# 24 short steps of spare transpositions among the last two backs, with another table of step orders, in a four-pair transformer kernel on one core

## The reference

```
x += L0_xattn(context)       one head
x += L0_ffn                  8 attention heads; their value and output products are
                             mixed from 8 experts a head, 2 of them with a gate above 0
x += L1_xattn(context)       16 heads of 8 columns, causal and length masks
x += L1_ffn                  ternary weights, gelu, layer norm inside
x += L2_xattn(context)       2 heads of 64, per-head norms, mask
x += L2_ffn                  8 experts of 256, best 2 by a softmax gate
x += L3_xattn(context)       16 heads of 64, with a bias
x += L3_ffn                  8 small experts, best 2 by group, and a shared branch
```

## Time and profile before

| | |
|---|---|
| median of 3 runs | 689.33 us (687.62 to 689.4) |
| the profiled execution's own time | 687.04 us |
| its span, first to last instruction | 685.7 us |
| mean granted TensorE clock | 0.979 of full |
| PE busy | 647.0 us (94%) |
| DVE busy | 521.0 us (76%) |
| ACT busy | 371.8 us (54%) |
| POOL busy | 201.1 us (29%) |
| DMA | 113.86 MB, mean 166 GB/s |

### The profile page before, as it was taken

The page is one execution under the profiler, slowest core; times in us unless marked ns, Lnnn a source line. Parts: engine busy times, 40 slices in busy tenths (PEclk is TensorE's granted clock), DMA queues, the critical chain, the costliest instruction groups (busy, mean ns, idle before and its releaser), DMA issues.

```text
span 685.7 us, 14701 instructions
## 1 busy us (share of the span) xinstructions
PE 647.0 (94%) x5494; PEld 582.2 (85%) x5494; DVE 521.0 (76%) x1433; ACT 371.8 (54%) x1261; POOL 201.1 (29%) x244
## 2 busy tenths in 40 slices
PE   6789999899999999999999999999999998788987
PEld 5669999798999999898799999878899987567866
DVE  1887678886888878987788898985688776556856
ACT  2252321355665846154665586386648452865693
POOL 0000012542251222513514242144336332432040
PEclk9799999999999999999999999999999999799989
DMA  8969969896324616895334126380565400000000
GB/s 317 393 233 302 391 237 322 282 363 208 136 93 139 205 47 212 262 325 195 129 124 161 65 65 246 127 275 14 179 232 178 150 9 5 1 1 1 1 1 13
DMA packets 37656, 113.86 MB, mean 166 GB/s; under 512 B 9041, under 2 KB 11729, under 8 KB 37201
## 3 DMA queue, kind: packets, MB, share of 16 engines
q1 hardware_dynamic: 37584, 112.92, 47.0%
HBM read 111.86 MB, written 1.05 MB: 165 GB/s over the span
## 4 chain that ended last, share of the span: by engine, by line
PE 80%; DVE 10%; ACT 4%; POOL 2%; DMA 2%; issue 1%; DVEq 0%
PE bank L461 34%; PE e_bank L461 33%; PE p_bank L461 5%; PE bank L706 4%; ACT wide_b L1129 1%; DVE gated L1435 1%; DMA gated<-gates_of 1%; PE bank L695 1%; DVE x L1438 1%; DVE wide_b L1438 1%; POOL wide_b L1339 1%; DVE f_route L1435 1%; ACT f_b L1038 1%; PE p_bank L561 1%; DVE max_neg L1721 1%
## 5 line engine op out<-in xcount | busy, mean ns | idle before, releaser
L461 PE MATMUL e_bank<-weights,gated 128*128 128x128 f32 x2048 | 245.2, 276 | 0.9 <-ACT f_a L988 0.7
L461 PEld LDWEIGHTS e_bank<-weights,gated 128*128 128x128 f32 x2048 | 236.2, 192 | 7.7 <-issue 3.0
L1129 ACT ACTIVATE wide_b<-wide_b,max_neg 128x120 f32<-128x120 f32 x272 | 103.5, 386 | 21.8 <-DVE max_neg L1721 15.2
L1339 POOL TENSOR_TENSOR wide_b<-wide_b,row_inv 128x480 f32<-128x480 f32 x64 | 75.2, 1180 | 135.1 <-DVE row_inv L1726 135.0
L1435 DVE TENSOR_TENSOR gated<-gated,f_v 128x1024 f32<-128x1024 f32 x64 | 80.0, 1272 | 10.8 <-ACT f_v L988 6.2
L1435 DVE TENSOR_TENSOR gated<-gated,f_xnT 128x1024 f32<-128x1024 f32 x64 | 80.9, 1286 | 5.4 <-DMA gated<-gates_of 4.8
L988 ACT ACTIVATE wide_a<-bank 120x512 f32<-120x512 f32 (+4 forms) x110 | 58.5, 542 | 41.4 <-PE bank L706 20.6
L1331 POOL TENSOR_TENSOR rstd<-var_eps,w_const 128x1 f32<-128x1 f32 (+1 forms) x48 | 32.0, 667 | 159.6 <-DVE var_eps L1431 159.6
L1129 ACT ACTIVATION_READ_ACCUMULATOR wide_b<-wide_b,max_neg 128x1 f32 x272 | 52.1, 192 | 0.0
L706 PE MATMUL bank<-w_const,wide_b 128*120 128x128 f32 x256 | 42.4, 297 | 5.9 <-POOL wide_b L1339 5.8
L1721 DVE TENSOR_REDUCE max_neg<-wide_b 128x4 f32<-128x480 f32 x64 | 41.8, 653 | 2.2
(11 more groups left out here) (263 smaller groups left out, 1208.5 us busy)
## 6 DMA issues: line engine op xcount, KB each, us to landing
gated<-gates_of SPq DMA_DIRECT2D x128, 512.0 KB, 6.0
weights<-in_experts SPq DMA_DIRECT2D x64, 512.0 KB, 6.5
w_L2f<-in_L2f SPq DMA_DIRECT2D x1, 2124.0 KB, 14.6
w_L3x<-in_L3x SPq DMA_DIRECT2D x1, 2108.0 KB, 18.5
wide_b<-in_raw0f SPq DMA_DIRECT2D x1, 1024.0 KB, 8.1
w_L3f<-in_L3f SPq DMA_DIRECT2D x1, 1000.0 KB, 20.8
w_L1f<-in_L1f SPq DMA_DIRECT2D x1, 516.0 KB, 10.6
x_next<-in_x SPq DMA_DIRECT2D x4, 128.0 KB, 4.0
```

Of the source, the lines that this page charges most:

```text
L461: return nc.tensor.matmul(o, lhsT, rhs, start=first, stop=last)
L1129: last = nc.scalar.activation(p, p, ACT.Exp, bias=max_neg[lane][:, h:h + 1], accum_out=row_sum[lane][:, h:h + 1])
L1339: nc.gpsimd.tensor_tensor(p3, p3, row_inv[lane][:, 4 * i:4 * i + 4].unsqueeze(2).broadcast_to([128, 4, K]), ALU.mult).then_inc(probs_norme ...
```

## The change

The TensorE front stream gets 25 further steps behind pair 3's front: one that waits for `e_x_ready` of pair 3, and 24 that each issue three transpositions of the identity into `e_bank`. Nothing reads them. The order table is replaced on all five engines.

```diff
+SPARE = 24
@@ TensorE, front_steps
                     for pair in range(PAIRS):
                         yield from front_pair(pair)
+                    pe.wait_ge(e_x_ready.sem, e_x_ready.upto(L0F, 1, PAIRS - 1))
+                    yield
+                    for _ in range(SPARE):
+                        for c in range(3):
+                            nc.tensor.transpose(e_bank[:, 128 * c:128 * c + 128], ident, ident)
+                        yield
@@ ORDER["PE"], from the last front product on
-1001010101110111011011001010101101101100100110001011100101100000000010101010010101110000101001011101101001110011
+1f0f1001001110ff1f1f11011011001010101101101f1fff001001010ff0f0f1f111001f01101000000000101010010101101f00f0100101f0f101101f1f110011f00ff11
@@ ORDER["SP"]
-"ppfffpffffffffffpfffffffffffffffffffffppfffffpffffffffffffffffffffffffpfffffffpfff0fffffpfffffffff1f"
-"ffffffff0fffffffpf1ff0ffffffffffff11f0ffpfff0fffffffffffffffff1ff0011f"
+"ppffpffffffffpffffffffffffffffffpffffpfffffffffffffpffffffffffffff0f1ffpffpfffffffffffffffffffpfff"
+"ffffffff10ffffff1fpffff0ffffpfffffffffffff0ffff1f1fffff0fffffff0011fff"
...
```

More of the change, by code:

```diff
@@ L43 @@
 ORDER = {
[L44 to L67, removed]
+    "PE": "pppp0pp00pp0pppp0pp00pp0pppp0pffpffpfpfffpfffpf0pffffpfpfpfpfpffffpfffffpffffpfffpp0p101p0pfffpf1f0f"
+          "f0fp10f0f0fp000p0f0f0fff01f00f0p10f0pfp0f0p0101f10p001010010110001pf0110p10f1010f10ff1p1f10ff100p1f1"
+          "101110101f01p10010111fp1ff1pfp001p110p101f0f1f01f1f0ff1f0pf11fff1p01ff1ff10pf1f0f1f01pf0f10010p1001p"
+          "11p01f10110f0011p11f1p10f0f11p100p0f1f01f001p001001000101010100f1p10f1f1011f01pf00f010p0100110101pf1"
+          "0fp01101f0f1010f1f1f01f10p10f00f0000f0f11f00f1001100f01f011001f10f11f0110010010101f00f110f010f0001f1"
+          "1f111101f11f101f111f0010f0101f0f10101101f111f0110ff1f0f1001001110ff1f1f11011011001010101101101f1fff0"
+          "01001010ff0f0f1f111001f01101000000000101010010101101f00f0100101f0f101101f1f110011f00ff11",
@@ new lines @@
+    "Activation": "ppppp0p0ppp0p0pp0pp0ppppppp0ppfp0pfp00fpfpf0pfpfppfpppp0ppp0p10pp10f00p10f00p00p00100f001ff10f00pf0p"
+          "fp11000p1101010101p010p11p100111001p1000p101001110100pp01010100p111p101p1p11p1101p1010f1011f01p1f0p1"
+          "00f1fp0f1f0f101110100011p01p01111011p1p11100p0101p1p0100p01001010010p010010p1p1001100100p01101001101"
+          "p10p01p01101110f100101f000001000010f1101110100p01f101100f1f110f10101001f1100011101110001011100010010"
+          "1111001111011011100110001100111111011010011100101011001110010100011010011000001010010100101000010010"
+          "110101110101100111101",
@@ new lines @@
+    "DVE": "pppppp0p0pppppp0p0pppppppppppppppfppfpfff0ffppffffppfffpffppfpfpppfpppfffpppfffffpfppfppffpfpppff0fp"
+          "pffp1ff0fff0001f0100ffp01ffff01fp00f1pp001010fff001f0pf0p0f0p00p01p010001f1001p0fp1ppf101p0f0p00101p"
+          "01pf11p1101pp1fppff11101f10f0p011p0110010011f10fppffpf0f1ffp0fffp0011ff0110111f1f1ff0p100ff1011p11ff"
+          "1f1p1ffp100p0011p0p10ff011f1ff1010pp10p1p10p0p1pf0110pp101p000p00100p011f1fp10010p0pf00f01101p1fp11p"
+          "1fpf01p0f0f00f00f0100f1110f11101f11f001f001000f10ff110ff10001ff1001f100011010011f0001f00101f00010f01"
+          "1ffff11011110110100011ff0f101f11f11f101ff0000010011111101110f01ff10001111110100100101111001010100101"
+          "010011101011100100001000001100000100111011101000000001111111101101",
@@ L68 @@
+    "Pool": "pppp000f011p111f0000f01000p010110110100100100100110111111f101f0p01100f011p11000111011010100101100010"
+          "0011f101100f01000001011110f0111010001001110110100111101f011011f1f1000011110001010100010000111011",
+    "SP": "ppffpffffffffpffffffffffffffffffffpffffpfffffffffffffpffffffffffffff0f1ffpffpfffffffffffffffffffpfff"
+          "ffffffff10ffffff1fpffff0ffffpfffffffffffff0ffff1f1fffff0fffffff0011fff",
 }
```

## The result

The changed kernel takes 684.11 us, median of 3 runs (684.04 to 684.84), against 689.33 (687.62 to 689.4): ratio 0.9935, 95% interval 0.9916 to 0.9953. A second measurement in the experiments gave 0.9926 (0.9901 to 0.995). The forecast was 687.8 us, 0.2% faster; the time lies in its range of 683.4 to 691.5, but the gain is three times as large, and most of it came where the forecast had 0.

What follows compares the result with a forecast made beforehand. TensorE's summed work bounds the kernel up to 577 us, two lanes' chains of short steps behind it. 687.04 - 1.0 - 0.4 - 0.3 + 0.2 + 0 = 685.5 us, 687.8 on the median's scale; range 683.4 to 691.5.

Steps and rivals of the forecast that it cites:

- The first part, "I take 0": New order up to 577 us: only waits can change, bounds -6.7 us and some us upward, taken as 0.
- the first 531 us win: Rival: TensorE's 6.7 us of waits in the first part shrink by 1 to 3 us, about 686 us; 12%.
- The order of the last backs, -1.7 in sum: New order in the last two backs: L2_ffn -1.0, L3_ffn -0.4, L1_xattn -0.3 us.
- The spares, +0.2 us: 24 spares in the last backs: 7.9 us of TensorE work, mostly in idle time, 0.2 us on the path.
- What the clock gives back, "I take 0 for both": Two low-clock stretches of the last backs, from 585 and 653 us: up to 3.7 us recoverable, taken as 0.
- the -0.3 forecast: L1_xattn, last backs: lane 0's fourth scores come before lane 1's transpositions, -0.3 us, bounds -1.15 and +1.3.
- The step on transpositions: Last backs: transpositions do not bring the fast clock, so spares hold nothing; without this rule up to 3.7 us more.
- L2_ffn, -1.0: Last backs: lane 1's o1 fills a TensorE wait, so lane 0's result is added 1.0 us sooner; bounds 0, -1.5.
- L3_ffn, -0.4: End of last backs: lane 1's top-2 step ahead of lane 0's sum on VectorE, -0.4 us; bounds 0, -1.0.
- The signs that I named: Right: two clock falls remain, TensorE's waits shrink about 7.9 us, first part within 1.5 us; wrong: it moves over 2 us.
- The clock holds: Rival: clock stays at the upper level in one or both last-back stretches, 1.2 to 3.7 us more, about 685; 15%.
- Spares exposed: Rival: 13 of 24 spares stand on the last backs' chain, 4.3 us, making the kernel 692.1 us; 8%.

Runs made afterwards that it cites:

- e2: Kernel before with its old order up to pair 3's front, then the changed last backs with spares; 0.9991 of before.
- e3: Changed order up to pair 3's front, then the last backs of the kernel before, no spares; 0.9947 of before.
- e4: Old order up to pair 3's front, changed order of the last backs, without the waiting step and 24 spares; 1.0015 of before.
- e11: Changed order up to about 480 us, order of the kernel before from there, no spares; 687.82 us, 0.9977 of before.
- e1: Changed kernel with its new order everywhere, but without the waiting step and the 24 spares; 0.9967 of before.
- e12: The changed kernel itself, unaltered, measured again beside other experiments; 684.25 us, 0.9926 of before.
- e5: Changed order up to pair 3's front, old order of the last backs with the wait and 24 spares put in; 1.0007 of before.
- e7: Changed kernel with six transpositions instead of three in each of the 24 spare steps; 688.75 us, 1.0015 of before.
- e6: Changed kernel with one float32 product of 192 columns in place of each spare's three transpositions; 684.61 us, 0.9946 of before.
- e10: Changed order up to pair 1's copy (about 264 us), order of the kernel before from there, no spares; 1.0076 of before.

## Why the prediction was right and wrong

**In short.** The time lies in the forecast's range, and that is luck. The forecast had its whole gain of 1.5 us in the last backs; there the change brought 0.6 us (e2, 0.1%, not told from nothing), and 3.6 us came from the first part, a term taken as 0. The range's lower end was drawn with the clock at its upper level in both stretches, which did not happen.

**What bounds the kernel.** Right: TensorE's sum up to 577 us, chains behind it.

**The first part, "I take 0".** This is the step that failed. e3 gives 3.6 us for it, and the trace 1.8. I had bounded it at -6.7 us from the sum of TensorE's waits and then looked at one queue, SP's, for what could get worse. Nothing was looked at for what could get better. A term with bounds of several us, on work of which most steps are moved, does not deserve a 0 with 12% for the rest. The rival "the first 531 us win" named it, at 1 to 3 us, a little under what e3 has. What makes the gain is shown in part only. The 1.8 us of the trace are 1.3 in the start-up, up to pair 0's copy, and 0.5 in pairs 1 to 3 together (454.1 us for 454.6, with 4.2 us of waits for 4.6). The start-up is no safe share: it takes 119.4 and 120.7 us in e2 and e4, which have the order of before, and 118.1 to 120.1 in the kernels with the changed one; the clock was at its lower level there in some and not in others of the same order (10.2 us of it in before, none in e2 and e4). What is sure is the stretch behind 480 us, 0.3% by e11 against e3, and one wait of 0.7 us in it. The rest of the 3.6 us stays open.

**The order of the last backs, -1.7 in sum.** Not borne out: without the spares it measured 1.0015 on the old first part (e4), and 0.2% above the old order on the new one (e1 against e3); neither is clear of nothing, and a gain of 1.7 us is in neither. In e4's trace, a short execution, L2 is 1.0 us shorter as forecast, while L1 is 0.2 and L3 0.2 us longer.

**The spares, +0.2 us.** Only half a step. Their cost in place was about right where a gap stands behind them; L3's 46.2 us against 45.5 in e4 make it 0.7 there. What failed is the thought that they are a cost alone: on the new order they are worth 0.24 to 0.4% (e2 against e4, e1 against both measurements of the changed kernel).

**What the clock gives back, "I take 0 for both".** Wrong in the middle: it was not all or nothing. The falls stayed, as forecast, and their stretches shrank by 3.4 us each. I had the wait for GpSimd shrinking from 3.36 to 1.5 to 2.5 us, and that was about right: it is 1.48 us in e12, 1.30 and 0.27 in e2, and hidden in the first trace by scores that ran at the lower clock. I had also put the wait ahead of the fall. In before the fall, at 585.4, stands inside the wait (583.8 to 587.2), and in the two traces of the changed kernel, at 582.7 and 584.4, ahead of it (in e12 it begins at 585.05). So in these two the fall did not come from that wait. L1 took 20.7 us for 21.9, for the -0.3 forecast; 0.5 us of this the old backs have too in e3 (21.4). Neither half does it: e4 has the scores moved and stays at 10.2 us, e5 has the spares and stays at 10.2 us. With both (e2, on e4's first part) the stretch is 6.8 us and L1 1.0 us shorter. The second stretch is 3.4 us in e4 too, without a spare.

**The step on transpositions.** The Trainium skill, page "TensorE: Matmul & The Clock Gate", section "Part 4: PE-mode transpose", has it that a transposition does not count as TensorE being busy in the same way. I had it that the trace does not contradict this, as the clock rose behind the products at 592.47. It rose at 595.7, and eight transpositions stand between:

```profile
594.32 1.72 PE L706 MATMUL bank<-w_const,wide_b 128*120 128x128 f32 x8
```

The changed kernel's traces contradict the rule. In the first one TensorE ran nothing but transpositions, spares and real ones, from 585.4 on (the timeline above), and the clock rose at 589.5, behind 4.1 us of them; in e7 it rose at 588.5, behind 3.8 us of them. e6 fits this: with products in place of the spare transpositions the time and both low stretches are the same. So for this kernel the measurement goes before the rule.

**L2_ffn, -1.0.** About right in the trace: 42.5 us for 43.3 with ten spares in it, 42.3 without them in e4 (43.4 in e1, whose clock fell once more, at 621).

**L3_ffn, -0.4.** Wrong: L3 to the end takes 0.9 us more, 0.2 without spares. VectorE's top-2 step is ahead as forecast, but lane 1's sum is then held by its experts' products and not by the gate, and lane 1's scores, now behind lane 0's transpositions, had no price in the sum.

**The signs that I named.** The two falls and the shrinking of TensorE's idle time (from 19.1 us behind 577 us to 11.0) came as written for a right forecast. The first part moved by 1.8 us, between the 1.5 of "right" and the 2 of "wrong".

**The rivals.** "The clock holds" came half true. "Spares exposed" was wrong for this order and right for e5 and e7, at 4.1 and 4.5 to 6 us, close to the 4.3 us it was priced at.

## What to carry to other kernels

A new order of a full engine deserves a term with bounds and a fair share of the chance, not a 0: the largest gain here came from the part that looked full. One trace a kernel would not have shown its size, as the old order's executions spread over 6 us. Before you compare two orders from milestone to milestone, count the instructions between them. In these runs filler on TensorE paid in the order that put it ahead of the instruction that waits, and cost time in the order that put it behind the wait, where it delays what the wait has held up already. And look at a wait in two executions before you call it gone. A change with two halves asks for all four corners (e1 to e4 and the change): only they showed that the half in the title brought 0.1%.

## What the runs showed of the hardware

- The stretches at the lower clock behind the copy came in five lengths: 3.4, 6.8, 10.2, 13.6 (e10) and 17.1 us (e1). How much TensorE waited in them does not tell the length: in those of 6.8 us it was busy for 6.8 (the changed kernel's first trace) but also for only 5.3 (e12, the same kernel).
- The clock rose behind 4.1 us (changed kernel) and 3.8 us (e7) in which TensorE ran only transpositions.
- In e10 the clock fell 1.3 us after TensorE had ended a wait of 2.83 us in a full stretch. With the 3.4 us that the low stretch cost, the wait was about twice as dear as the list of waits shows.
- With TensorE busy for 89.44 of 98.0 us the clock was at 1.00 through all of them (e7), and the kernel was slower than with 3.4 us more at the lower clock.
- A spare of three transpositions took 0.33 us at the full clock (e7, six in 0.65 us from 589.40) and 0.67 us at half (changed kernel, six in 1.34 us from 585.36).
- The spread of a kernel's runs went with the order behind 480 us: 4.3 to 6.3 us with the old one (before, e2, e4, e10, e11), 1.7 to 2.7 us in six runs and more with the changed one, but for e1 (4.5 us, no spares). One thing that moved is seen: in e2 TensorE waits 1.8 us for GpSimd in pair 2 where before and e4, in the same order, wait 0.8. Whether it makes the spread is not settled.
